# Counting edges in 55 steps of 12 destinations instead of 40 steps of 16

## The reference, cut to what matters

```
# layer 0: attention over the edges
h = x @ W
e = exp(-leaky_relu(al[src] + ar[dst]))
h_prime = segment_sum(e * h[dst], src) / (segment_sum(e, src) + EPS)
x1 = layernorm(x + elu(h_prime))
# layer 1: eight relations
u = x1 @ root + bias
for r in range(8):
    mean_r = segment_sum(x1[src] * (edge_type == r), dst) / max(count_r, 1)
    u = u + mean_r @ weight[r]
z = concat([u, x1]) @ w_gate + b_gate
out = layernorm(x1 + tanh(u) * z + x1 * (1 - z))
```

## Time and profile before

| | |
|---|---|
| time, median of three runs | 995.83 us |
| the profiled execution | 996.23 us |
| its span, first to last instruction | 994.2 us |
| TensorE busy in the span | 980.8 us (99%) |
| VectorE busy | 391.7 us (39%) |
| ScalarE busy | 281.3 us (28%) |
| mean granted TensorE clock | 0.998 of 2.4 GHz |

### The profile page before, as it was taken

How to read it: one execution, slowest core, us unless ns; L and a number is a source line. 1 busy time by engine, 2 the same in 40 slices (tenths; PEclk the granted TensorE clock), 3 DMA queues, 4 the chain that set the end, 5 groups by cost and what they waited for, 6 DMA issues and landing times.

```text
span 994.2 us, 14628 instructions
## 1 busy us (share of the span) xinstructions
PE 980.8 (99%) x5159; PEld 825.1 (83%) x5159; DVE 391.7 (39%) x746; ACT 281.3 (28%) x487; POOL 254.3 (26%) x196
## 2 busy tenths in 40 slices
PE   9999999999999999999999999999999999999997
PEld 7866778788888888888888988988988988888886
DVE  7998773720332330430530440242232233202277
ACT  4325543741122122221221221222222212212432
POOL 0000002065323223223223132142232232326730
PEclk9999999999999999999999999999999999999999
DMA  7304657066211411411311321231141051212402
GB/s 265 95 13 119 177 143 239 1 225 199 79 40 33 154 41 42 141 51 42 131 62 42 108 84 42 74 118 33 27 165 33 20 170 34 73 52 66 138 1 103
DMA packets 69005, 91.41 MB, mean 92 GB/s; under 512 B 9396, under 2 KB 35475, under 8 KB 68838
## 3 DMA queue, kind: packets, MB, share of 16 engines
q1 hardware_dynamic: 68966, 90.90, 29.1%
HBM read 75.19 MB, written 15.69 MB: 91 GB/s over the span
## 4 chain that ended last, share of the span: by engine, by line
PE 94%; DVE 2%; ACT 1%; issue 1%; DVEq 0%; POOL 0%; ACTq 0%
PE ps L1188 21%; PE ps L1190 21%; PE ps L1189 21%; PE ps L1444 9%; PE ps L1443 9%; PE ps L1294 5%; PE ps L1256 1%; PE ps L1499 1%; PE ps L1498 1%; PE ps L1497 1%; PE ps L1269 1%; PE ps L1277 1%; PE ps L1271 1%; PE ps L1270 1%; PE ps L1432 0%
## 5 line engine op out<-in xcount | busy, mean ns | idle before, releaser
L469 POOL TENSOR_TENSOR w_lo<-w_raw,w_hi 128x512 fp32r<-128x512 f32 x168 | 217.4, 1299 | 697.9 <-ACT w_hi L544 546.6
L544 ACT CAST w_hi<-w_raw 128x512 fp32r<-128x512 f32 x184 | 114.7, 623 | 464.9 <-PE ps L1190 397.2
L1188 PE MATMUL ps<-w_hi,M_hi 128*128 128x512 f32 (+1 forms) x550 | 215.9, 393 | 0.1
L1190 PE MATMUL ps<-w_lo,M_hi 128*128 128x512 f32 (+1 forms) x550 | 214.6, 390 | 0.0
L1189 PE MATMUL ps<-w_hi,M_lo 128*128 128x512 f32 (+1 forms) x550 | 214.5, 390 | 0.0
L1062 DVE SCALAR_TENSOR_TENSOR u<-ps,scale,u 128x512 f32<-128x512 f32 (+1 forms) x90 | 66.4, 744 | 314.8 <-PE ps L1190 314.8
L1443 PE MATMUL ps<-C_hi,x_hi 128*128 128x320 f32 (+3 forms) x640 | 184.5, 306 | 0.0
L1444 PE MATMUL ps<-C_hi,x_lo 128*128 128x320 f32 (+3 forms) x640 | 184.4, 307 | 0.0
L1188 PE MATMUL ps<-w_hi,M 128*128 128x512 f32 (+1 forms) x360 | 140.4, 390 | 0.0
L1190 PE MATMUL ps<-w_lo,M 128*128 128x512 f32 (+1 forms) x360 | 140.4, 390 | 0.0
L1189 PE MATMUL ps<-w_hi,M 128*128 128x512 f32 (+1 forms) x360 | 140.4, 390 | 0.0
(11 more groups left out here) (178 smaller groups left out, 773.6 us busy)
## 6 DMA issues: line engine op xcount, KB each, us to landing
w_raw<-weights SPq DMA_DIRECT2D x184, 256.0 KB, 2.8
C_dram<-Cst SPq DMA_DIRECT2D x25, 512.0 KB, 6.3
C_hi<-C_dram SPq DMA_DIRECT2D x8, 1600.0 KB, 7.0
z<-b_gate SPq DMA_DIRECT2D x5, 512.0 KB, 9.6
u<-bias SPq DMA_DIRECT2D x5, 512.0 KB, 7.5
xT_raw<-xT SPq DMA_DIRECT2D x8, 312.5 KB, 6.5
u<-x SPq DMA_DIRECT2D x4, 512.0 KB, 4.9
last_raw<-weights SPq DMA_DIRECT2D x8, 256.0 KB, 5.6
```

The source lines that it names most:

```text
L469: pool.tensor_tensor(w_lo[k % RING][:, :], w_raw[k % RING][:, :], w_hi[k % RING][:, :].bitcast(f32), ALU.subtract).then_inc(w_lo_done, 1)
L544: nc.scalar.copy(w_hi[k % RING][:, :], w_raw[k % RING][:, :]).then_inc(w_hi_done, 1)
L1188: mm(o, lhs_hi[:, k, c], w_hi[k % RING][:, :], start=opens, stop=False)
L1190: last = mm(o, lhs_hi[:, k, c], w_lo[k % RING][:, :], start=False, stop=closes_)
```

## The change

A window is now 12 destinations wide, so that 40 codes times 12 destinations are 480 columns and fit one bank: one matmul of 480 columns for each tile. A block of 128 destinations takes 11 windows, ten of 12 and one of 8, and there are 55 windows in all. A pass has four tiles, `hot` four slots. The windows take banks 5 and 6 by turns from the first one on, and one zero matmul opens a window. `win_edge` is worked out in more steps, since a block's start is no multiple of 12. `MULT_W[j]` becomes `PER * (j + 1) + 6`, which for `PER` = 8 is what stood there before.

```diff
--- before.py
+++ after.py
@@ -27,16 +27,17 @@
     FLT_MAX = 3.4028234e38
 
     TILES = dst_cols.shape[1]
-    BODY = 5
+    BODY = 4
     ALL_TILES = -(-TILES // BODY) * BODY
     STARTS = ALL_TILES - BODY + 1
     LOOP_END = STARTS * (ALL_TILES // BODY)
     SUB = 2
     UNITS = dst_units.shape[0]
-    WIN = P // R
-    WINDOWS = NP // WIN
-    PER = P // WIN
     CODES = NT * R
+    WIN = 512 // CODES
+    PER = -(-P // WIN)
+    WINDOWS = NT * PER
+    HOT = CODES * WIN
     SPLIT = NP // 2
     NE = N + N % 2
     NCOL = [(0, 320), (320, NE - 320)]
@@ -48,6 +49,12 @@
     ITEMS = 1 + 2 * KT
     GB = 3
     SUMS = 2 * KT
+
+    def win_at(w):
+        return P * (w // PER) + WIN * (w % PER)
+
+    def win_width(w):
+        return min(WIN, P - WIN * (w % PER))
 
     def rows(t):
         return P if t < NT - 1 else N - P * (NT - 1)
@@ -132,7 +139,7 @@
                 iota_body = sb("iota_body", [P, ALL_TILES // BODY], f32, setup)
                 reach = sb("reach", [WINDOWS, 2, SUB * UNITS], f32, setup)
             att16 = sb("att16", [P, RING_A, NP], i16, early)
-            hot = sb("hot", [P, BODY * NP], bf16, early)
+            hot = sb("hot", [P, 5 * NP], bf16, early)
             all_r = sb("all_r", [P, PART_S * P], f32r, early)
             with ExitStack() as dotting:
                 a_bc = sb("a_bc", [P, 2 * D], f32, dotting)
@@ -316,18 +323,13 @@
         E_W, MULT_W = [], []
         for j in range(NT):
             E_W.append(max(AL_W + 2 + 2 * j, MULT_W[j - 2] + 2 if j >= 2 else 0))
-            MULT_W.append(max(E_W[j] + 4, PER * j + 14))
+            MULT_W.append(max(E_W[j] + 4, PER * (j + 1) + 6))
 
         def hp_w(j):
             return MULT_W[j] + 3 if j < NT - 2 else WINDOWS
 
-        TWINS = AL_W + 2
-
         def window_bank(w):
-            return 2 if w >= TWINS and (WINDOWS - w) % 2 == 0 else 5
-
-        def last_in_pair(w):
-            return max([v for v in range(w) if window_bank(v) == window_bank(w)], default=-1)
+            return 5 + w % 2
 
         PE_ENGINE, DVE_ENGINE = mybir.EngineType.PE, mybir.EngineType.DVE
 
@@ -452,7 +454,7 @@
 
         @block.gpsimd
         def _(pool):
-            pool.iota(iota_i[:, :], pattern=[[1, CODES], [P // 2, WIN]], base=0, channel_multiplier=0).then_inc(pool_consts, 1)
+            pool.iota(iota_i[:, 0:HOT], pattern=[[1, CODES], [P // 2, WIN]], base=0, channel_multiplier=0).then_inc(pool_consts, 1)
             pool.iota(part_col[:, :], pattern=[[0, 1]], base=0, channel_multiplier=1,
                       allow_small_or_imprecise_dtypes=True).then_inc(pool_consts, 1)
             pool.iota(iota_s[:, :], pattern=[[1, P]], base=0, channel_multiplier=0,
@@ -572,15 +574,13 @@
 
             def copy_window(w):
                 j, v = divmod(w, PER)
+                n = win_width(w)
                 act.wait_ge(window_counted, w + 1)
                 if v == 0 and j >= 2:
                     act.wait_ge(flushed[j - 2], 16 * NT)
                     act.wait_ge(turned, 2 * (j - 1))
-                nc.scalar.copy(Cst[j % 2][:, :, :, v * WIN:(v + 1) * WIN].rearrange("p m r d -> p (m r) d")
-                               .rearrange("p (b q) d -> p b q d", b=2),
-                               ps[:, window_bank(w) * H2:(window_bank(w) + 2) * H2]
-                               .rearrange("p (b n) -> p b n", b=2)[:, :, 0:SPLIT]
-                               .rearrange("p b (q d) -> p b q d", d=WIN)).then_inc(window_copied, 1)
+                nc.scalar.copy(Cst[j % 2][:, :, :, v * WIN:v * WIN + n].rearrange("p m r d -> p (m r) d"),
+                               bank(window_bank(w), c=HOT).rearrange("p (q d) -> p q d", d=WIN)[:, :, 0:n]).then_inc(window_copied, 1)
 
             def copy_summed(j, part):
                 m0, m1 = turn_blocks(part)
@@ -805,10 +805,15 @@
             v.memset(y_sq[:, :], 1.0)
             step(v.memset(dots[:, :], 0.0))
             dve.wait_ge(pool_consts, 6)
-            v.tensor_scalar(table[:, :], iota_i[:, :], 1.0 / (P // 2), None, ALU.mult)
+            v.tensor_scalar(table[:, 0:HOT], iota_i[:, 0:HOT], 1.0 / (P // 2), None, ALU.mult)
             v.tensor_scalar(ident_r[:, :], iota_s[:, :], part_col[:, :], None, ALU.is_equal)
             v.tensor_scalar(win_edge[:, 0:1], part_col[:, :], float(WIN), None, ALU.mult)
-            step(v.tensor_scalar(win_edge[:, 1:2], part_col[:, :], float(WIN), float(WIN - 1), ALU.mult, ALU.add))
+            step(v.tensor_scalar(win_edge[:, 1:2], part_col[:, :], float(PER), float(P - PER * WIN), ALU.is_ge, ALU.mult))
+            for j in range(1, NT):
+                step(v.tensor_tensor(win_edge[:, 0:1], win_edge[:, 0:1], win_edge[:, 1:2], ALU.add))
+                if j < NT - 1:
+                    step(v.tensor_scalar(win_edge[:, 1:2], part_col[:, :], float(PER * (j + 1)), float(P - PER * WIN), ALU.is_ge, ALU.mult))
+            step(v.tensor_scalar(win_edge[:, 1:2], win_edge[:, 0:1], float(WIN - 1), None, ALU.add))
             def split_low(n, k):
                 dve.wait_ge(w_hi_done, 8 * n + k + 1)
                 v.tensor_tensor(w_lo[k % RING][:, :], w_raw[k % RING][:, :], w_hi[k % RING][:, :].bitcast(f32),
@@ -940,7 +945,7 @@
                 tile = dve.snap(tile_at, min_val=0, max_val=ALL_TILES - BODY)
                 for s in range(BODY):
                     dve.wait_ge(counted[s], n)
-                    v.tensor_scalar(hot[:, s * NP:(s + 1) * NP], table[:, :], float(WIN * w),
+                    v.tensor_scalar(hot[:, s * HOT:(s + 1) * HOT], table[:, 0:HOT], float(win_at(w)),
                                     key[:, ds(tile + s, 1)], ALU.add, ALU.is_equal).then_inc(built[s], 1)
                 dve.reg_add(turn, turn, 1)
                 dve.reg_add(tile_at, tile_at, BODY)
@@ -1290,11 +1295,8 @@
                 edge = pe.snap(edge_at, min_val=0, max_val=(ALL_TILES - BODY) * P)
                 for s in range(BODY):
                     pe.wait_ge(built[s], n)
-                    for c in range(2):
-                        last = mm(bank(window_bank(w) + c, c=SPLIT), oh_s[:, ds(edge + s * P, P)],
-                                  hot[:, s * NP + c * SPLIT:s * NP + (c + 1) * SPLIT],
-                                  start=False, stop=False, skip_group_check=True)
-                    last.then_inc(counted[s], 1)
+                    mm(bank(window_bank(w), c=HOT), oh_s[:, ds(edge + s * P, P)], hot[:, s * HOT:(s + 1) * HOT],
+                       start=False, stop=False, skip_group_check=True).then_inc(counted[s], 1)
                 pe.reg_add(turn, turn, 1)
                 pe.reg_add(edge_at, edge_at, BODY * P)
 
@@ -1302,14 +1304,11 @@
                 first_pass = window_range(PE_ENGINE, w)
                 pe.reg_mod(edge_at, first_pass, STARTS)
                 pe.reg_mul(edge_at, edge_at, P)
-                pe.wait_ge(window_copied, last_in_pair(w) + 2)
-                if w == TWINS + (WINDOWS - TWINS) % 2:
-                    pe.wait_ge(u_drained, 2 * NT + 4)
-                for c in range(2):
-                    mm(bank(window_bank(w) + c, c=2), zeros[:, :], zeros[:, 0:2], start=True, stop=False, skip_group_check=True)
+                pe.wait_ge(window_copied, max(w, 1))
+                mm(bank(window_bank(w), c=2), zeros[:, :], zeros[:, 0:2], start=True, stop=False, skip_group_check=True)
                 with pe.Fori(first_pass, LOOP_END, STARTS + BODY):
                     counts(w)
-                mm(bank(window_bank(w) + 1, c=2), zeros[:, :], zeros[:, 0:2], start=False, stop=True, skip_group_check=True)\
+                mm(bank(window_bank(w), c=2), zeros[:, :], zeros[:, 0:2], start=False, stop=True, skip_group_check=True)\
                     .then_inc(window_counted, 1)
 
                 for k, t in items(w):
```

## The result

The changed kernel takes 1009.33 us (four runs, 1008.72 to 1009.54), the kernel before in the same series 995.64. The ratio is 1.0133, with a 95% interval from 1.0120 to 1.0145: 13.7 us slower, where 6.4 were forecast. The direction and the place were right, the forecast size was less than half of what came, and the time lies outside the forecast's range.

A forecast was written before the change was run, and what follows sets the result against it. TensorE's chain bounds the kernel, with its sequencer's serial work per window setting the pace in bare windows. Array work -9.3, window ends -0.3 and holes +16.0 gave +6.4 us on 995.83: 1002.2 us, range 999 to 1007.

The forecast's parts named there:

- The array terms, -9.3 and -0.3: Counting matmuls: 59 passes of 0.81 us replace 42 of 1.36, -9.3 us; window ends (zeros and close), -0.3 us.
- Holes after: 24.8 us: TensorE's holes in the counting stage after the change: 24.8 us against 8.8 before, +16.0 us.
- w = 0 to 7: First windows, with two items each: the second pass of w = 1 waits for rebuilding; 0.7 us of holes.
- w = 8 to 11: Nothing else stands on TensorE there, so it waits for VectorE three times; 3.8 us of holes.
- w = 12 to 14: The broadcast on TensorE covers most of the waiting; 0.3 us of holes.
- 22 bare windows: Windows with nothing between them: sequencer needs 1.5 us, array 0.87, hole 0.63 each; 14.7 us together.
- three groups of sums and turns: Windows 22 to 25, 33 to 36, 44 to 47: holes of 1.65 us each, 5.0 in all (bounds 1.8 and 7).
- around attention: Holes around the attention matmuls, which come two windows earlier, at 20, 31 and 42: 0.3 us.
- (A): Counting stage: the array sets the time, sequencer work stays hidden; holes stay 8.8, 986.2 us; chance 0.11.
- (B): Same sequencer chain, cheap end: 1.37 us a bare window, short loads behind turns; 996.1 us, no change; chance 0.08.
- (C): VectorE becomes the bound: builds stay at 0.295 us, bare windows take 1.7; 1007.6 us; chance 0.06.
- (D): TensorE's clock falls because the array rests more in bare windows; 10 to 20 us, near 1017; chance 0.03.

The follow-up runs named there:

- Experiment 5: Changed kernel with each flush writing the counts of relation 0 alone, an eighth of the data: 1004.30 us, ratio 1.0079.
- Experiment 1: Changed kernel with tile ranges written in as constants and passes written out, no register work on TensorE and VectorE: 993.69 us, ratio 0.9979.
- experiment 9: Changed kernel with fixed tile ranges, VectorE building only 240 of a slot's 480 columns: 987.21 us, ratio 0.9916.
- experiment 3: Changed kernel with a second load of each window's number on TensorE alone: 1026.87 us, ratio 1.0308.
- experiment 4: Changed kernel with a second load of each window's number on VectorE alone: 1018.42 us, ratio 1.0236.
- experiment 7: Changed kernel with one load of 11 numbers at each block's first window instead of one number per window: 1010.36 us, ratio 1.0136.
- experiment 10: Changed kernel with all windows in bank 5, each waiting for the copy of the one before: 1032.92 us, ratio 1.0363.
- experiment 12: Changed kernel with grouped loads placed at windows 0, 7, 16, 27, 38 and 49: 1014.80 us, ratio 1.0188.
- experiment 2: Kernel before with the ranges of its 40 windows written in as constants and passes written out: 989.94 us, ratio 0.9939.
- experiment 8: Kernel before with one load of 8 numbers at each block's first window: 995.04 us, ratio 0.9987.
- experiment 11: Kernel before with grouped loads placed at windows 0, 4, 12, 20, 28 and 36: 993.29 us, ratio 0.9974.

## Why the forecast was wrong, point by point

**Right.** The mechanism (the sequencer's serial work per window), the sign, the number of passes, the matmul spacing (0.81 us for four, forecast 0.808), the builds (0.254, forecast 0.255), the windows with items (2.31 to 2.35 in w = 4 to 7, forecast 2.35), bare windows (1.55, forecast 1.5), slot waits 0.12 to 0.13 and 1.05 us between passes, three waits for `hot` in w = 9 to 11, the start at no cost, nothing moved after the stage. The array terms, -9.3 and -0.3, hold: the counted work is 51.1 us.

**The step that failed is "Holes after: 24.8 us".** They are 114.7 - 51.1 - 32.4 = 31.2. With the 8.8 before, the sum is -9.6 + 22.4 = +12.8 us instead of +6.4. By its terms:

| stretch | holes forecast | measured |
|---|---|---|
| w = 0 to 7 | 0.7 | 0.8 |
| w = 8 to 11 | 3.8 | 4.0 |
| w = 12 to 14 | 0.3 | 1.8 |
| 22 bare windows | 14.7 | 16.3 |
| three groups of sums and turns | 5.0 | 7.0 |
| around attention | 0.3 | 1.2 |

(The other 0.1 is rounding.) The largest miss is the groups, 2.35 us each where 1.65 were set. Their term was 1.05 behind the first turn, 0.3 ahead of the second and "0.3 to 1.0" behind it, and the sum took the 0.3, as if the load there were short. The first part came out (0.7 ahead of the zeros and 0.3 ahead of the products), but behind the second turn the loads took 1.00, 0.63 and 1.02 us and left holes of 0.9, 0.5 and 0.9. The upper bound given for these groups, 7, was the right value. Experiment 5 shows the cause of the holes: with no long loads the groups are 5.4 shorter, which is the part that the forecast had and the part that it left out together. The groups are 2.0 of the 6.4 us missed; the other 4.4 are spread over w = 12 to 14 (1.5), the bare windows (1.6), the windows around attention (0.9) and small amounts.

In w = 12 to 14 the broadcast covers the first turn, but not what comes next. TensorE's timeline, then ScalarE's:

```profile
83.84 1.18 PE L1261 MATMUL ps<-Cst,ident 128*128 128x256 f32 x8 [0.42 <-ACT att L596]
...
85.46 2.14 PE L1298 MATMUL ps<-hot,oh_s 128*128 128x480 bf16 x8
```

```profile
82.70 0.62 ACT L546 CAST w_hi<-w_raw 128x512 fp32r<-128x512 f32 x1
83.22 0.48 ACT L596 CAST att<-ps 128x384 int16<-128x384 f32 x1
```

The second sum waits for ScalarE's copy of the first turn, which stands behind a split of weights; then come 0.3 ahead of the zeros of w = 14, behind a load of 1.03 us, 0.3 ahead of the products, and 0.4 between the two passes of w = 14 (2.03 us from 85.46 to the close at 87.49, against 1.62 of array work). The forecast priced none of them. The wait for ScalarE is 0.42 us in experiments 1 and 5 too, so neither the registers nor the long loads make it; that the split of weights does is the trace's reading alone, and no run varied it.

In the bare windows 22 times 0.05 is 1.1 of the 1.6 us; w = 52 with its two passes, 0.4 instead of 0.2, and the 0.6 that the first of them were to save and did not (w = 15 and 16 took 1.74 and 1.70 us) make up the rest.

The median moved by 13.7 us, the profiled span by 12.6. The four runs of after had a mean clock of 0.999 (the profiled one) and 0.996 to 0.997 (the others), so in the others the clock was a little lower somewhere; where was not seen. The sum had no term for that. But the profiled execution of after lies 0.6 us under its median and that of before 0.6 over the median of its runs here, so the 1.1 us between the two measures are no more than the scatter of both kernels.

**The rivals.** (A), the array sets the time: refuted; holes grew by 22 us. It is what experiment 9 comes close to, 987.2 us against 986.2, after two other limits are gone. (B), the cheap end: refuted, the loads behind the turns are the long ones. (C), VectorE becomes the bound: not in this kernel (1.6 us of waits), but it is the next limit. Experiment 1 shows it, and it is why the change, with no register work in either kernel, would still be slower, 993.69 against 989.94. The forecast held VectorE's bound only as an alternative to the sequencer's, with one condition, the price of a build; that price was as forecast and VectorE was still nearly the bound. (Its 1.3 to 1.4 us for VectorE's loop does not follow from its own terms either: 1.71 less 0.295 and 0.16 is 1.26.) (D), the clock falls: not in the profiled execution (1.00 throughout the stage). Yet in experiments 1, 3, 4, 5, 7, 10 and 12 the clock was between 0.50 and 0.97 in stretches of 10 us or so. That was nearer than the rows of before, all at 1.00, let the forecast see.

The two limits overlap, so their parts do not add up by themselves. Holes were 8.8 before and 3.1 in experiment 2; 31.2 after and 16.1 in experiment 1. The change therefore adds 13.0 of holes that are there without register work, most of them by VectorE's pace, and 9.4 more by registers, against 9.6 of array work saved.

## What to carry to other kernels

Where an engine loads a register, computes and goes round a loop for each small piece of work, price the piece on its sequencer, and do it with the load's duration in the place where it will stand: beside a large write-out it was three times as long, unless array work stood there to cover it. Splitting work into more pieces multiplies the fixed part, so compare it with the array's saving per piece first (1.0 us a window against 9.6 us in all, here). And remove one limit on paper and look for the next: two engines within 0.5 us of each other leave little to win.

## What the runs showed of the hardware

- A register load of one number took 0.30 us at rest and 0.97 to 1.03 beside the write-out of 2.5 MB. The Trainium skill's floor of about 600 ns (DMA: Bandwidth & Descriptors, section "Latency and other measured facts") holds for one number in none of the quiet stretches.
- A load of several numbers is not priced by their count. With little or no transfer beside it (DMA share 0.12 at most), 8 numbers took 0.59 to 0.60 us (experiments 8 and 11), 9 numbers 2.18 (experiment 12), and 11 numbers 1.32, 1.33, 2.63 and 2.81 (experiments 7 and 12). Before the stage, at w = 0, 7 numbers took 1.25 us and 8 took 0.78. The short ones of the first list start at a place in the row that is a multiple of four numbers (windows 4, 8, 12, 16, 24, 32, 44), the long ones do not (7, 22, 33); that this is the reason is a guess from these few loads, which no run tested. Beside a write-out, 8 numbers took up to 1.95 and 11 numbers up to 5.6.
- The granted clock stayed at 1.00 in windows that rest 0.25 to 0.31 us ahead of the zeros and some 0.15 ahead of the products in each 1.55, and through single rests of 0.71 and 0.74 (the changed kernel, profiled). With 0.68 us of rest ahead of the zeros of every window it was still 1.00 at windows 26 to 28, and fell to 0.50 in later stretches (experiment 10). The Trainium skill (TensorE: Matmul & The Clock Gate, section "A second HAM failure mode: psum-queue depth-cycling") ties such a fall to cycling through PSUM banks. Here that does not sort the runs: the changed kernel and experiments 3, 7 and 12 all alternate two banks, and the first kept its clock while the others fell to between 0.55 and 0.97 in stretches, and experiment 10, which stays in one bank, fell the furthest.
- VectorE's build of 480 columns repeated after 0.254 us against 0.295 for 640: a quarter less width gave 14% less time.
